# Linear-attention block on one core: out products of the full and the pooled half issued by turns, and the next-but-one strip's convolution moved between the kv products

## The chip, the core and the metric

One Trainium2 chip, one of its cores. The metric is the device time of one execution in microseconds (us). The kernel before takes 805.83 us, the median of three runs (805.62 to 808.54). All arithmetic is fp32.

## What is computed

The input x has shape (4, 128, 96, 96). It is normalised by group (32 groups of 4 channels) and then goes through a linear attention over 4x4 windows. Cut to what matters:

```python
qkv = einsum('nchw,oc->nohw', xw, qkv_w)            # xw: windows of 4x4 pixels of the normalised x
pooled = avg_pool5(qkv)                             # 5x5 mean inside the 4x4 window, zero padded
msq = concatenate([qkv, pooled], axis=1)            # a "full" half and a "pooled" half, 16 heads of 8 each
q, k, v = relu(msq[..., :8]), relu(msq[..., 8:16]), msq[..., 16:]    # v gets a ninth column of ones
kv  = einsum('ngld,nglm->ngdm', k, v)               # the kv products, 8 x 9 for each window and head
out = einsum('ngld,ngdm->nglm', q, kv)              # the out products
out = out[..., :-1] / (out[..., -1:] + 1e-15)
y = einsum('nchw,oc->nohw', out, proj_w)            # the projection of both halves
y = y * inv + shift                                 # batch norm
result = x + y
```

Pooling a 4x4 window by 5x5 leaves only 3x3 different values, so the kernel keeps 9 pixels of a window in the pooled half.

## The kernel before, in words

The image is cut into 96 strips of 4 rows (24 windows, 384 pixels, 216 pooled pixels). A strip s goes through these steps. Each bears the name of the helper in the code, and its engine:

- GpSimd (POOL), `normalise_and_pool(s)`: subtracts the mean (line 289), multiplies by 1/std (line 294, `xn_ready`) and adds up the 3x3 pooled sums (line 267, `xp_ready`). It waits for `q_p` of strip s-2, since `xn` and `xp` have two buffers each.
- TensorE (PE): `conv_kv(s)` (line 681) and `conv_kv_pooled(s)` (line 690) make k and v, `conv_q_full(s)` (line 706) and `conv_q_pooled(s)` (line 716) make q, all of them on the whole 128x128 array. `kv_products(s)` and `kv_products_pooled(s)` (both line 728) use tiles of 64x64 of the array. The out products (line 740) use tiles of 64 rows by 32 columns: 48 matmuls for each half, and the profile records every fp32 matmul as two MATMUL and two LDWEIGHTS. `project_full(s)` (line 797) and `project_pooled(s)` (line 805) are again on the whole array.
- ScalarE (ACT): `relu_q`, `relu_q_pooled` (line 384), `masked_v_full`, `masked_v_pooled` (line 365), `relu_k`, `relu_k_pooled` (lines 347 and 348) move the convolutions out of PSUM with relu and masks, `copy_y_pooled` (line 407) takes the pooled projection.
- VectorE (DVE): `own_heads` (line 565) masks the kv products into `kvc_full` and `kvc_pool`, `divide` (lines 594, 595, 598) divides the out products, `turn` (line 607) transposes them, `residual` (line 571) adds the full projection to x. On 72 of the strips it also takes the statistics of two strips of the next image (line 459).
- GpSimd again, `residual_pooled(s)` (line 267): adds the pooled projection; then the SyncE queue stores the strip.

PSUM has eight banks and is full: bank 6 holds the pooled k and v (`KV_P`), and later the full q (`Q_F`); bank 7 holds the pooled q and the pooled out products; the pooled kv products use banks 4 and 5, and bank 5 also holds the full out products. So `conv_kv_pooled` waits until ScalarE has read the full q of the strip before (`qm_f`), and `kv_products_pooled` waits until `divide` has read the full out products (`num_f`).

Every engine works through a fixed order, written by hand, one step per strip. On TensorE, step s of the kernel before is

```python
conv_kv(s + 1, p); conv_kv_pooled(s + 1, p); project(s - 1, out_next=True)
out_products(s); out_products_pooled(s)
kv_products(s + 1); kv_products_pooled(s + 1); conv_q(s + 1, p)
```

Strip 0 and the last one are written out, the others run in a hardware loop of two steps. On the other engines all 96 steps are written out. In a tile of the out products the rows come from the quad j of a half (64 partitions), the columns from the quad i of the output: i = 2g + j, so that the four matmuls of a window pair go to tiles (rows 0, columns 0), (rows 1, columns 1), (rows 0, columns 2), (rows 1, columns 3), in units of 64 rows and 32 columns.

Of the kernel before, what the change touches and what calls it, by code (L numbers as in the profile page):

```python
# [73 lines left out]
def build(nc, x, wq, wkv, proj, bn, consts, out):  # L74
# [24 lines left out]
    with ExitStack() as ctx:  # L99
        def sb(name, shape):  # L100
            return ctx.enter_context(nc.sbuf_tensor(name, [P, *shape], F32))
# [124 lines left out]
        def is_first(s):  # L226
            return isinstance(s, int) and s == 0
# [108 lines left out]
        def _(act):  # L336
# [18 lines left out]
            def relu_k_pooled(s):  # L355
                act.wait_ge(conv_p, s + 1)
                wait(act, kv_p, s)
                masked_k(k_pool, kv_tiles(KV_P, TP)[:, :, 0:P], C_KP).then_inc(km_p, 1)
# [9 lines left out]
            def masked_v_full(s, pairs=range(EF)):  # L368
                act.wait_ge(conv_f, s + 1)
                wait(act, kv_f, s)  # L370
                last = masked_v(vm_full, kv_tiles(KV_F, TF)[:, :, P:], pairs, C_VF)
                if EF - 1 in pairs:
                    last.then_inc(vm_f, 1)

            def masked_v_pooled(s):
                act.wait_ge(conv_p, s + 1)
                wait(act, kv_p, s)
                masked_v(vm_pool, kv_tiles(KV_P, TP)[:, :, P:], range(EP), C_VP).then_inc(vm_p, 1)
# [39 lines left out]
            def step(s, b, at, phase):  # L418
                if not is_first(s):
                    relu_q(s)  # L420
                    relu_q_pooled(s)
                if not is_first(s) and not is_last(s):
                    masked_v_full(s + 1)
                    relu_k(s + 1)
                if not is_last(s):
                    relu_k_pooled(s + 1)
                if not is_first(s):
                    copy_y_pooled(s - 1)
                if not is_last(s):
                    masked_v_pooled(s + 1)  # L430
                if phase == 3:
                    square_root(b + 1)

# [15 lines left out]
        def _(dve):  # L449
# [16 lines left out]
            def channel_stats(b):  # L466
                chained(dve.bn_aggr(mv[:, 0:2], stats[:].rearrange("p n c -> p (n c)")), b, 1)
# [88 lines left out]
            def own_heads(s, pooled):  # L556

                ready, free, done, bank, kvc = (
                    (kv_p, out_p, kvc_p, KVP, kvc_pool) if pooled else (kv_f, out_f, kvc_f, KVF, kvc_full))
                dve.wait_ge(ready, s + 1)  # L560
                wait(dve, free, s)
                shape = [P, 2, HALF, KC]
                own = col(C_OWN, KC).unsqueeze(1).unsqueeze(1).to_broadcast(shape)
                src = ps[:, bank:bank + 2, 0:HALF * KC].rearrange("p r (w c) -> p r w c", c=KC)
                dve.tensor_tensor(kvc[:], src, own, ALU.mult).then_inc(done, 1)  # L565

            def residual(s):
                dve.wait_ge(y_f, s + 1)
                xs = x_all[:, s * SP:(s + 1) * SP].rearrange("p (r w c) -> p r w c", r=WS, c=WS)
                ys = ps[:, Y_F, 0:SP].rearrange("p (w r c) -> p r w c", r=WS, c=WS)  # L570
                dve.tensor_tensor(xs, ys, xs, ALU.add).then_inc(added_f, 1)  # L571
# [29 lines left out]
            def turn(s, pooled):  # L601
                done, free, turned, o, o_t = (
                    (num_p, y_p, turned_p, o_pool, o_pool_t) if pooled else (num_f, y_f, turned_f, o_full, o_full_t))
                dve.wait_ge(done, s + 1)

                wait(dve, free, s)
                dve.transpose(o_t[:].rearrange("p n j -> p (n j)"),
                              o[:].rearrange("p n j -> p (n j)")).then_inc(turned, 1)

            def step(s, b, at, phase):  # L610
                own_heads(s, False)
                if phase == 0:
                    dve.wait_ge(gathered, b * FOURS + FOURS)
                own_heads(s, True)
                if is_first(s):
                    dve.wait_ge(proj_turned, 1)
                    dve.tensor_copy(projT[:], ps[:, PROJ_T, 0:2 * P]).then_inc(projT_ready, 1)
                if at is not None:
                    dve.wait_ge(loaded_later, 16 * (((b - 1) * SPB + at) // 2 + 1))
                    gather_strip(b, at)  # L620
                    last = gather_strip(b, at + 1)
                    if at % 4:
                        last.then_inc(gathered, 1)
                if phase == 0:
                    channel_stats(b)
                elif phase == 1:
                    group_average(b, 1)
                elif phase == 2:
                    group_mean(b)
                    group_average(b, 8)  # L630
                elif phase == 3:
                    group_var(b)
                elif phase == 4:
                    group_rstd(b, b + 2)
                if not is_first(s) and not is_last(s):
                    residual(s - 1)
                divide(s, False)
                if is_last(s):
                    turn(s, False)
                divide(s, True)  # L640
                if not is_last(s):
                    turn(s, False)
                turn(s, True)
                if is_last(s):
                    residual(s - 1)

            dve.wait_ge(loaded_w, 16 * 5)
            for e in range(EF):
# [13 lines left out]
            setup(dve.tensor_tensor(shift[:], bn_sb[:, 1:2], bn_off[:], ALU.subtract))  # L662
            dve.tensor_scalar(proj_sb[:], proj_sb[:], bn_inv[:], None, ALU.mult).then_inc(proj_scaled, 1)

            over_strips(step)
            residual(NS - 1)
            residual_pooled_last()

        @block.tensor
        def _(pe):  # L670
# [59 lines left out]
                                             start=True, stop=True)  # L730
                return last

            def out_products_of(q, kvc, bank, pairs):

                for n in range(HALF):
                    half, e = divmod(n, pairs)
                    for g in range(G):
                        for j in range(QG):
                            i, rows, z = g * QG + j, slice(H64 * j, H64 * (j + 1)), QS + n * QS + g * Q4
                            last = pe.matmul(ps[Q4 * i:Q4 * (i + 1), bank, n * KC:(n + 1) * KC], q[rows, z:z + Q4],  # L740
                                             kvc[rows, half % 2, (half // 2 * G + g) * pairs + e],
                                             start=True, stop=True)
                return last

            def kv_products(s):
# [29 lines left out]
                    pe.wait_ge(qm_p, s + 1)  # L775

            def out_products(s):
                if is_first(s) or is_last(s):
                    out_wait(s)
                    pe.nop(nofuse=True)  # L780
                out_products_of(q_full, kvc_full, OUTF_LAST if is_last(s) else OUTF, EF).then_inc(out_f, 1)

            def out_products_pooled(s):

                if is_last(s):
                    pe.wait_ge(kvc_p, s + 1)
                    pe.nop(nofuse=True)
                out_products_of(q_pool, kvc_pool, OUTP, EP).then_inc(out_p, 1)

            def project_full(s):  # L790
                pe.wait_ge(turned_f, s + 1)
# [20 lines left out]

            def step(s, p):

                if not is_first(s):
                    conv_kv(s + 1, p)
                    conv_kv_pooled(s + 1, p)
                    project(s - 1, out_next=True)
                out_products(s)
                out_products_pooled(s)  # L820
                if is_first(s):

                    pe.wait_ge(projT_ready, 1)
                kv_products(s + 1)
                kv_products_pooled(s + 1)
                conv_q(s + 1, p)

# [15 lines left out]
                last = pe.transpose(ps[:, PROJ_T, z * P:(z + 1) * P], proj_sb[:, z * P:(z + 1) * P], col(C_IDENT, P))  # L843
            last.then_inc(proj_turned, 1)


            step(0, 1)
            with pe.Fori(1, NS - 1, 2) as s:
                step(s, 0)
                step(s + 1, 1)  # L850
            out_products(NS - 1)
            project_full(NS - 2)
            out_products_pooled(NS - 1)
            project_pooled(NS - 2)
            project(NS - 1)


# [29 lines left out]
```

## Time and profile before

| | |
|---|---|
| median of three runs | 805.83 us |
| the profiled execution | 805.22 us |
| its span, first to last instruction | 803.4 us |
| TensorE clock granted, mean | 0.995 |
| busy: TensorE / VectorE / GpSimd / ScalarE | 766.7 / 622.8 / 591.6 / 567.4 us |
| one strip in the steady part | 7.91 us |

A group's time on TensorE is best read from the start of its first instruction to the start of the next group's first one, since matmuls overlap. "Idle before <-releaser" tells what an engine waited for; "issue" is a wait that the profile shows no cause for.

### The profile page before, as it was taken

Reading aid. Unit: us, or ns where it says so; the run is one execution under the profiler, and the core shown is the slowest. Engines: PE = TensorE matmul, PEld = TensorE weight load, DVE = VectorE, ACT = ScalarE, POOL = GpSimd, SP = SyncE. Lnnn points to the kernel's source line nnn. Section 1 sums busy time; section 2 is a strip of 40 time slices with the busy share of each in tenths; the row PEclk is TensorE's granted clock in tenths of the full one; section 3 lists DMA queues with packets and bytes.
Section 4 is the critical chain, followed back from the end, with each engine's and each line's share of the span. In section 5 each row is a group of like instructions: output and inputs, shape, how many; then the busy total and the mean of one; then the engine's idle time right before and its main releaser. Section 6 shows DMA issues by size and latency. Waiting matters only on the chain. (4 is left out here: it accounts for less than half of the span.)

```text
span 803.4 us, 62585 instructions
## 1 busy us (share of the span) xinstructions
PE 766.7 (95%) x28226; PEld 669.6 (83%) x28226; DVE 622.8 (78%) x1250; ACT 567.4 (71%) x1350; POOL 591.6 (74%) x1336
## 2 busy tenths in 40 slices
PE   0879999999999999999999999999999999999995
PEld 0668888888888888888888888888888888888884
DVE  7857888887768888888767888888777776767675
ACT  0557776768676777777676767677777767676773
POOL 0557877778787878787787878787877778787861
PEclk9999999999999999999999999999999999999998
DMA  7022131000012232000012222100000000000000
GB/s 298 3 63 59 59 89 40 30 29 21 29 59 82 66 89 59 30 20 30 23 47 70 77 75 74 49 20 29 20 30 20 30 26 24 30 20 30 20 30 31
DMA packets 20643, 38.74 MB, mean 48 GB/s; under 512 B 2416, under 2 KB 15216, under 8 KB 20592
## 3 DMA queue, kind: packets, MB, share of 16 engines
q1 hardware_dynamic: 20592, 38.25, 14.7%
q14 instruction: 42, 0.34, 0.1%
q8 instruction: 9, 0.15, 0.1%
HBM read 19.36 MB, written 18.87 MB: 48 GB/s over the span
## 5 line engine op out<-in xcount | busy, mean ns | idle before, releaser
L384 ACT ACTIVATE q_full<-ps,cst 128x384 f32<-128x384 f32 x192 | 103.7, 591 | 200.2 <-PE ps L706 200.2
L289 POOL TENSOR_TENSOR xd<-x_all,mean_t 128x384 f32<-128x384 f32 x95 | 78.8, 829 | 139.1 <-PE ps L716 119.3
L681 PE MATMUL ps<-wkv_sb,xn 128*128 128x256 f32 x576 | 142.9, 384 | 22.3 <-DVE xn L521 22.3
L267 POOL TENSOR_TENSOR x_all<-y_pool,x_all 128x96 f32<-128x96 f32 x380 | 148.2, 426 | 16.2 <-ACT y_pool L407 16.2
L681 PEld LDWEIGHTS ps<-wkv_sb,xn 128*128 128x128 f32 x576 | 102.9, 192 | 32.5 <-issue 22.3
L365 ACT ACTIVATE vm_pool<-ps,cst 128x256 f32<-128x256 f32 x288 | 119.5, 524 | 0.0
L571 DVE TENSOR_TENSOR x_all<-ps,x_all 128x384 f32<-128x384 f32 x96 | 53.5, 557 | 80.1 <-PE ps L797 80.0
L740 PEld LDWEIGHTS ps<-kvc_full,q_full 64*32 64x32 f32 x9216 | 88.1, 106 | 27.3 <-issue 27.3
L365 ACT ACTIVATE vm_full<-ps,cst 128x384 f32<-128x384 f32 x192 | 101.0, 579 | 4.6 <-PE ps L681 4.6
L740 PE MATMUL ps<-kvc_pool,q_pool 64*32 64x36 f32 x9216 | 100.3, 198 | 3.6 <-issue 3.6
L740 PE MATMUL ps<-kvc_full,q_full 64*32 64x36 f32 x9216 | 99.0, 198 | 1.5 <-ACT q_pool L384 1.5
L565 DVE TENSOR_TENSOR kvc_pool<-ps,cst 128x864 f32<-128x864 f32 x96 | 99.9, 1041 | 0.4 <-PE ps L728 0.4
L690 PE MATMUL ps<-wkv_sb,xp 128*128 128x256 f32 x384 | 99.0, 380 | 0.0
L565 DVE TENSOR_TENSOR kvc_full<-ps,cst 128x864 f32<-128x864 f32 x96 | 97.9, 1020 | 0.7 <-PE ps L728 0.7
L728 PE MATMUL ps<-vm_full,k_full 64*64 64x72 f32 x4608 | 95.2, 227 | 3.2 <-issue 3.2
L740 PEld LDWEIGHTS ps<-kvc_pool,q_pool 64*32 64x32 f32 x9216 | 90.8, 105 | 4.5 <-issue 4.4
L267 POOL TENSOR_TENSOR hs<-ht,xn 128x96 f32<-128x96 f32 x190 | 83.6, 440 | 14.9
L728 PE MATMUL ps<-vm_pool,k_pool 64*64 64x108 f32 x3072 | 89.3, 254 | 0.0
L706 PE MATMUL ps<-xn,wq_sb 128*128 128x192 f32 x384 | 89.3, 356 | 0.0
L728 PEld LDWEIGHTS ps<-vm_full,k_full 64*64 64x64 f32 x4608 | 80.5, 133 | 7.9 <-issue 3.5
L294 POOL TENSOR_TENSOR xn<-xd,rstd_t 128x384 f32<-128x384 f32 x95 | 78.5, 827 | 7.5
L690 PEld LDWEIGHTS ps<-wkv_sb,xp 128*128 128x128 f32 x384 | 73.0, 191 | 10.4 <-DVE xp L514 0.4
(72 smaller groups left out, 1414.6 us busy)
## 6 DMA issues: line engine op xcount, KB each, us to landing
out<-x_all SPq DMA_DIRECT2D x96, 192.0 KB, 1.9
x_all<-x SPq DMA_DIRECT2D x36, 384.0 KB, 3.3
x_all<-x SPq DMA_DIRECT2D x6, 768.0 KB, 8.2
wkv_sb<-wkv SPq DMA_DIRECT2D x1, 128.0 KB, 10.8
wq_sb<-wq SPq DMA_DIRECT2D x1, 128.0 KB, 10.6
proj_sb<-proj SPq DMA_DIRECT2D x1, 128.0 KB, 10.5
cst<-consts SPq DMA_DIRECT2D x1, 90.0 KB, 10.9
bn_sb<-bn SPq DMA_DIRECT2D x1, 2.0 KB, 10.3
```

What stands on the lines that cost most here:

```text
L267: return pool.tensor_tensor(o, a, b, ALU.add)
L289: link(pool.tensor_tensor(xd[:], x_all[:, s * SP:(s + 1) * SP], mean, ALU.subtract), 1)
L294: pool.tensor_tensor(xr, rows, rstd, ALU.mult).then_inc(xn_ready, 1)
L365: last = act.activation(heads[:, e, :, :, 0:D], src, ACT.Copy, scale=col(masks + e))
L384: return act.activation(to, src, ACT.Relu, scale=col(mask))
L565: dve.tensor_tensor(kvc[:], src, own, ALU.mult).then_inc(done, 1)
L571: dve.tensor_tensor(xs, ys, xs, ALU.add).then_inc(added_f, 1)
L681: last = pe.matmul(ps[:, bank, at:at + 2 * P], xn[:, p, t * P:(t + 1) * P], wkv_sb[:], start=True, stop=True)
L690: last = pe.matmul(ps[:, KV_P, t * 2 * P:(t + 1) * 2 * P], xp[:, p, t * P:(t + 1) * P], wkv_sb[:], start=True, stop=True)
L706: last = pe.matmul(ps[:, bank, PX + r * SP // PAIR:PX + (r + 1) * SP // PAIR], wq_sb[:, r], full[:, r], start=True, stop=True)
L728: last = pe.matmul(ps[H64 * j:H64 * (j + 1), bank + r, (t * G + g) * n:(t * G + g + 1) * n], k[rows, t, at:at + H64], vm[rows, :, t, i * K ...
L740: last = pe.matmul(ps[Q4 * i:Q4 * (i + 1), bank, n * KC:(n + 1) * KC], q[rows, z:z + Q4], kvc[rows, half % 2, (half // 2 * G + g) * pairs ...
```

## The change

1. The out products of both halves are issued by turns: the four matmuls of a window pair in the full half, then the four of the pooled half. The pooled ones have the two quads of a half swapped in their output place (i = 2g + 1 - j), so that they go to the four tiles that the full ones leave free; the columns of the projection weights are permuted to match, on the host. Both semaphores, `out_f` and `out_p`, are set at the end.
2. TensorE's step s is put in another order. `conv_kv` now runs for strip s+2 and stands between the full and the pooled kv products; `conv_kv_pooled(s + 2)` stands between the two projections of strip s.
3. ScalarE: `masked_v_full` runs for strip s+2, at the end of the step; `copy_y_pooled` comes ahead of `relu_k_pooled`.
4. VectorE: `divide` full, `divide` pooled, `own_heads(s+1)` full, `turn` full, `own_heads(s+1)` pooled, `turn` pooled, `residual(s)`; the statistics stand at the start of the step.
5. The hardware loop ends two strips earlier; the steps of strips 93 and 94 are written out.

```diff
-                    masked_v_full(s + 1)
                     relu_k(s + 1)
-                if not is_last(s):
-                    relu_k_pooled(s + 1)
                 if not is_first(s):
                     copy_y_pooled(s - 1)
                 if not is_last(s):
+                    relu_k_pooled(s + 1)
                     masked_v_pooled(s + 1)
+                if s < NS - 2:
+                    masked_v_full(s + 2)
...
+            def step(s, b, at, phase):
+                statistics(b, at, phase)
                 divide(s, False)
                 if is_last(s):
                     turn(s, False)
                 divide(s, True)
                 if not is_last(s):
+                    own_heads(s + 1, False)
                     turn(s, False)
+                    own_heads(s + 1, True)
                 turn(s, True)
-                if is_last(s):
-                    residual(s - 1)
+                residual(s)
...
+            def out_pair(q, kvc, bank, pairs, n, swap):
+                half, e = divmod(n, pairs)
+                for g in range(G):
+                    for j in range(QG):
+                        i, rows, z = g * QG + (1 - j if swap else j), slice(H64 * j, H64 * (j + 1)), QS + n * QS + g * Q4
...
             def out_products(s):
+                for n in range(HALF):
+                    full = out_pair(q_full, kvc_full, OUTF, EF, n, False)
+                    pooled = out_pair(q_pool, kvc_pool, OUTP, EP, n, True)
+                    if n == HALF - 1:
+                        full.then_inc(out_f, 1)
+                        pooled.then_inc(out_p, 1)
...
             def step(s, p):
-                if not is_first(s):
-                    conv_kv(s + 1, p)
-                    conv_kv_pooled(s + 1, p)
-                    project(s - 1, out_next=True)
+                convolved = not isinstance(s, int) or s < NS - 2
                 out_products(s)
-                out_products_pooled(s)
                 kv_products(s + 1)
+                if convolved:
+                    conv_kv(s + 2, p)
                 kv_products_pooled(s + 1)
-                conv_q(s + 1, p)
+                conv_q(s + 1, 1 - p)
+                project_full(s)
+                if convolved:
+                    conv_kv_pooled(s + 2, p)
+                project_pooled(s, out_next=True)
...
-            step(0, 1)
-            with pe.Fori(1, NS - 1, 2) as s:
-                step(s, 0)
-                step(s + 1, 1)
+            step(0, 0)
+            with pe.Fori(1, NS - 3, 2) as s:
+                step(s, 1)
+                step(s + 1, 0)
+            step(NS - 3, 1)
+            step(NS - 2, 0)
```

## Rows read from the trace of the kernel before

**Rows 1.** The page: busy time of each engine, its share of the span, instructions.
```profile
PE 766.7 (95%) x28226; PEld 669.6 (83%) x28226; DVE 622.8 (78%) x1250; ACT 567.4 (71%) x1350; POOL 591.6 (74%) x1336
```

**Rows 2.** Timeline, TensorE, one strip: start us, us, engine, line, operation, count.
```profile
400.44 0.92 PE L706 MATMUL ps<-xn,wq_sb 128*128 128x192 f32 x4
401.19 0.59 PE L716 MATMUL ps<-xp,wq_sb 128*128 128x108 f32 x4
401.62 1.47 PE L681 MATMUL ps<-wkv_sb,xn 128*128 128x256 f32 x6
402.93 1.03 PE L690 MATMUL ps<-wkv_sb,xp 128*128 128x256 f32 x4
403.80 0.81 PE L797 MATMUL ps<-o_full_t,projT 128*128 128x384 f32 x2
404.44 0.53 PE L805 MATMUL ps<-o_pool_t,projT 128*128 128x216 f32 x2
404.91 1.01 PE L740 MATMUL ps<-kvc_full,q_full 64*32 64x36 f32 x95
...
405.74 1.02 PE L740 MATMUL ps<-kvc_pool,q_pool 64*32 64x36 f32 x95
406.69 0.98 PE L728 MATMUL ps<-vm_full,k_full 64*64 64x72 f32 x48
407.50 0.92 PE L728 MATMUL ps<-vm_pool,k_pool 64*64 64x108 f32 x32
408.35 0.92 PE L706 MATMUL ps<-xn,wq_sb 128*128 128x192 f32 x4
```

**Rows 3.** Timeline cut at 404.96 (weight loads) and at 405.5 (matmuls).
```profile
404.90 0.15 PEld L740 LDWEIGHTS ps<-kvc_full,q_full 64*32 64x32 f32 x8 [0.27 <-issue]
404.91 0.78 PE L740 MATMUL ps<-kvc_full,q_full 64*32 64x36 f32 x68
```

**Rows 4.** Timeline, TensorE, before strip 0's out products.
```profile
28.17 0.98 PE L728 MATMUL ps<-vm_full,k_full 64*64 64x72 f32 x48
29.09 1.56 PE L681 MATMUL ps<-wkv_sb,xn 128*128 128x256 f32 x6
30.58 0.97 PE L728 MATMUL ps<-vm_pool,k_pool 64*64 64x108 f32 x32
31.48 1.13 PE L690 MATMUL ps<-wkv_sb,xp 128*128 128x256 f32 x4
32.45 0.38 PE L843 MATMUL ps<-cst,proj_sb 128*128 128x128 f32 x2
```

**Rows 5.** Timeline, ScalarE, the strip of rows 2.
```profile
401.39 1.08 ACT L384 ACTIVATE q_full<-ps,cst 128x384 f32<-128x384 f32 x2 [2.02 <-PE ps L706]
402.36 0.82 ACT L384 ACTIVATE q_pool<-ps,cst 128x216 f32<-128x216 f32 x2
```

**Rows 6.** Timeline, a TensorE instruction that waited for ScalarE, at the end.
```profile
797.37 0.44 ACT L407 ACTIVATE y_pool<-ps,shift 128x216 f32<-128x216 f32 x1 [6.77 <-issue]
...
797.96 1.21 PE L797 MATMUL ps<-o_full_t,projT 128*128 128x384 f32 x2 [2.48 <-ACT y_pool L407]
```

**Rows 7.** Timeline, VectorE, the strip of rows 2 and on.
```profile
405.98 0.21 DVE L594 TENSOR_SCALAR den_full<-ps 128x48 f32<-128x48 f32 x1 [0.78 <-PE ps L740]
...
407.18 0.20 DVE L594 TENSOR_SCALAR den_pool<-ps 128x48 f32<-128x48 f32 x1
...
408.38 0.57 DVE L607 STREAM_TRANSPOSE o_full_t<-o_full 128x384 f32<-128x384 f32 x1
...
409.33 1.02 DVE L565 TENSOR_TENSOR kvc_full<-ps,cst 128x864 f32<-128x864 f32 x1
...
410.27 1.04 DVE L565 TENSOR_TENSOR kvc_pool<-ps,cst 128x864 f32<-128x864 f32 x1
```

**Rows 8.** Timeline, TensorE, code of strip 0's step, then out products around the loop's end.
```profile
37.33 0.34 PE L728 MATMUL ps<-vm_full,k_full 64*64 64x72 f32 x4 [1.54 <-issue]
...
784.43 1.01 PE L740 MATMUL ps<-kvc_full,q_full 64*32 64x36 f32 x95
...
798.96 0.93 PE L805 MATMUL ps<-o_pool_t,projT 128*128 128x216 f32 x2
```

More of the change, by code:

```diff
@@ L608, in turn, with statistics @@
                               o[:].rearrange("p n j -> p (n j)")).then_inc(turned, 1)
[L610 to L617, printed above, removed]
+            def statistics(b, at, phase):
                 if at is not None:
@@ L624, in step @@
                 if phase == 0:
+                    dve.wait_ge(gathered, b * FOURS + FOURS)
                     channel_stats(b)
@@ L634, in step @@
                     group_rstd(b, b + 2)
-                if not is_first(s) and not is_last(s):
-                    residual(s - 1)
+            def step(s, b, at, phase):
+                statistics(b, at, phase)
                 divide(s, False)
@@ L641, in step @@
                 if not is_last(s):
+                    own_heads(s + 1, False)
                     turn(s, False)
+                    own_heads(s + 1, True)
                 turn(s, True)
-                if is_last(s):
-                    residual(s - 1)
+                residual(s)
             dve.wait_ge(loaded_w, 16 * 5)
@@ L663, in _ @@
             dve.tensor_scalar(proj_sb[:], proj_sb[:], bn_inv[:], None, ALU.mult).then_inc(proj_scaled, 1)
+            own_heads(0, False)
+            own_heads(0, True)
+            dve.wait_ge(proj_turned, 1)
+            dve.tensor_copy(projT[:], ps[:, PROJ_T, 0:2 * P]).then_inc(projT_ready, 1)
             over_strips(step)
-            residual(NS - 1)
             residual_pooled_last()
@@ L731, in kv_tile @@
                 return last
[L733 to L742, printed above, removed]
+            def out_pair(q, kvc, bank, pairs, n, swap):
[3 more added lines that the diff above has]
+                        i, rows, z = g * QG + (1 - j if swap else j), slice(H64 * j, H64 * (j + 1)), QS + n * QS + g * Q4
+                        last = pe.matmul(ps[Q4 * i:Q4 * (i + 1), bank, n * KC:(n + 1) * KC], q[rows, z:z + Q4],
+                                         kvc[rows, half % 2, (half // 2 * G + g) * pairs + e],
+                                         start=True, stop=True)
                 return last
@@ L777, in out_products, with out_products_last @@
             def out_products(s):
-                if is_first(s) or is_last(s):
+                if is_first(s):
                     out_wait(s)
                     pe.nop(nofuse=True)
-                out_products_of(q_full, kvc_full, OUTF_LAST if is_last(s) else OUTF, EF).then_inc(out_f, 1)
-            def out_products_pooled(s):
-                if is_last(s):
-                    pe.wait_ge(kvc_p, s + 1)
-                    pe.nop(nofuse=True)
-                out_products_of(q_pool, kvc_pool, OUTP, EP).then_inc(out_p, 1)
+                for n in range(HALF):
[4 more added lines that the diff above has]
+                        pooled.then_inc(out_p, 1)
+            def out_products_last(s, pooled):
+                if pooled:
+                    pe.wait_ge(kvc_p, s + 1)
+                else:
+                    out_wait(s)
+                pe.nop(nofuse=True)
+                for n in range(HALF):
+                    last = (out_pair(q_pool, kvc_pool, OUTP, EP, n, True) if pooled else
+                            out_pair(q_full, kvc_full, OUTF_LAST, EF, n, False))
+                last.then_inc(out_p if pooled else out_f, 1)
             def project_full(s):
@@ L844, in _ @@
             last.then_inc(proj_turned, 1)
-            step(0, 1)
-            with pe.Fori(1, NS - 1, 2) as s:
-                step(s, 0)
-                step(s + 1, 1)
[L851 to L854, printed above, removed]
+            step(0, 0)
[4 more added lines that the diff above has]
+            step(NS - 2, 0)
+            out_products_last(NS - 1, False)
+            out_products_last(NS - 1, True)
             project(NS - 1)
@@ L869 @@
     wq = np.stack([quads, quads[:, ::-1]], axis=1).transpose(0, 1, 3, 2, 4).reshape(P, PAIR, P)
-    proj = np.asarray(L0_conv_proj_w).reshape(P, 2 * P)
+    proj = np.asarray(L0_conv_proj_w).reshape(P, 2, G, QG, Q4).copy()
+    proj[:, 1] = proj[:, 1, :, ::-1]
+    proj = np.ascontiguousarray(proj.reshape(P, 2 * P))
     arrays = {
```

## The prediction

> **What bounds the kernel now.** I read the page's busy shares first, then one strip of the timeline engine by engine, then the first strips. TensorE is busy for 95% of the span and no other engine for more than 78% [rows 1]. In a strip of 7.91 us (from one conv_q at 400.44 to the next at 408.35) its groups follow each other without a hole [rows 2]: conv_q 0.75 and 0.43, conv_kv 1.31, its pooled half 0.87, the projections 0.64 and 0.47, the out products 0.83 and 0.95, the kv products 0.81 and 0.85. ScalarE waits 2.02 us in the same strip for TensorE, and VectorE at least 0.78 [rows 5, 7]. So a strip costs what TensorE's own chain costs, and the change pays if that chain gets shorter. It must not put a wait into it.
>
> **The out products by turns.** From the first record to the last they take 1.66 us for 192 matmul records (404.91 to 406.57; the last start is the kv products' start at 406.69 less a hand-over of 0.13) [rows 2]. That is 8.6 ns a record, while only four of the eight 64x32 tiles work. With all eight in turn a record no longer waits for its own tile, and what is left is how fast records come. Two rows bound that. At the start of the group eight weight loads go out in 0.055 us, with four matmuls among them: about 6.7 ns for a load and its matmul [rows 3]. That burst is the fastest in the trace; at its pace 192 records take 1.30 us with the start-up. The other bound is today's 1.66. After the burst the first 68 records have gone by 405.5, 8.7 ns each, and the other 124 take the remaining 1.07 us, 8.6 ns each [rows 2, 3]: it never again comes near 6.7. The loads, far ahead of the matmuls in the first slice (eight loads to five matmuls), have no lead worth the name later. An engine that waits for a tile would have its loads done ahead; one that waits for instructions would look like this. So I take the supply of instructions as the limit of the long part, and from the extra tiles only the gain in the first part: 1.60 us, a gain of 0.06 us a strip. That nothing is gained is the upper bound (1.66), 1.30 the lower one of this reading.
>
> The Trainium skill speaks for more. Its page "TensorE: Matmul & The Clock Gate", Part 3, has matmuls on different tiles start about 4 ns apart, by which 192 records would take 0.77 us. No stretch of this trace goes at that pace, and the fastest one has 6.7 ns; it is one of the rivals below.
>
> **The new place of conv_kv.** Between the two kv products the array changes from 64x64 tiles to the whole array and back, which the kernel before does not do in the steady part. But it does so once, ahead of strip 0 [rows 4]: full kv 28.17, conv_kv 29.09, pooled kv 30.58, next group 31.48. There the full kv products cost 0.91 where a steady strip has 0.81, conv_kv 1.49 against 1.31, the pooled kv products 0.90 against 0.85 [rows 2, 4]. The sum is 0.34 us a strip more. None of it hides, since TensorE is the chain. It could be less if some of those 0.18 us in conv_kv were a wait for VectorE's or ScalarE's first-strip work; I put its lower bound at 0.2.
>
> **The new place of conv_kv_pooled.** It still waits for `qm_f`, both parts of relu_q, because it writes bank 6. Today conv_q pooled (0.43) and conv_kv (1.31) stand between conv_q_full and it; afterwards conv_q pooled and project_full (0.64). TensorE gets to it 0.75 + 0.43 + 0.64 = 1.82 us after conv_q_full starts. relu_q starts 0.95 us after conv_q_full starts (400.44 to 401.39) and takes 1.08 [rows 2, 5]: 2.03 us. The hand-over from ScalarE to TensorE took 0.15 us where TensorE waited for it (797.81 to 797.96) [rows 6]. So conv_kv_pooled starts at 2.18 instead of 1.82: a new wait of 0.36 us in every strip. Behind an empty array the group also takes longer: conv_kv_pooled took 0.97 (31.48 to 32.45) after a change of tiles against 0.87 [rows 2, 4], 0.10 more. Together 0.45 us. Queued behind it are the pooled projection and the next out products; relu_q_pooled, which the pooled projection waits for, ends at 402.36 + 0.82 = 403.18, 2.74 us after conv_q_full, and conv_kv_pooled (0.87 after 2.18, so 3.05 and more) covers it [rows 5].
>
> **What doesn't bind.** VectorE now has divide full, divide pooled and one own_heads ahead of the full turn. A divide takes 1.20 us from start to start (405.98, 407.18, 408.38), the two turns 0.95, an own_heads 0.94 [rows 7]. After the last out record: 0.24 + 1.20 + 1.20 + 0.94 + 0.57 + 0.1, that is 4.25 us to project_full. TensorE gets there after 0.13 + 0.91 + 1.49 + 0.90 + 0.75 + 0.43 = 4.61. To the pooled projection VectorE needs 0.24 + 2.40 + 1.88 + 0.95 + 0.1 = 5.6, TensorE 4.61 + 0.64 + 0.36 + 0.97 = 6.6. The full divide (1.5 us to its end, to be done before the pooled kv products) is covered by full kv and conv_kv, 2.5 us. ScalarE works 5.9 us in a strip, moves masked_v_full into its idle time ahead of relu_q and is free there; GpSimd's strip is unchanged and starts from `q_p` as before, with xn ready 1.8 us later and needed after about 5. Were one of these covers gone, its cost would be the difference of the two numbers named. These edits I cost at nothing.
>
> **Edges.** Strips 93 and 94 are now straight code. Strip 0's step, also straight code, lost 1.54 us in the middle of its kv products to nothing the profile names but issue [rows 8]; for two such steps I add 3.2 us (bounds 0 and 8). In the tail of the kernel before, the last pooled projection starts 14.5 us after strip 94's out products (784.43 to 798.96) [rows 8]. In the new order VectorE's chain sets it, about 7.7 us to the last out products and 5 behind them: 1.5 us less.
>
> **The sum.** Per strip +0.34 + 0.45 - 0.06 = +0.73 us, so 8.64 us a strip. It applies to some 92 strips (1 to 93, less one for the first pass through the loop's code, where other waits cover it): +67.4. With the edges (+3.2 - 1.5) it is +69.1. The profiled execution of before takes 805.2 us, 0.6 below the median, so it gives 874.3 as a profiled execution and **875** as a median.
>
> **The rivals.**
> - Records come at the burst's pace all through (6.7 ns). For it: the burst exists and eight tiles free the array. Against: 8.6 ns later without the loads' lead. Out products 1.30: +0.43 x 92 + 1.7 = +41, **847**.
> - The new wait does not appear, because relu_q starts earlier or bank 6 is free sooner than I read. For it: only that its size, 0.45, is a difference of longer terms. +0.28 x 92 + 1.7 = +27, **833**.
> - The turns do nothing at all: two tiles in the same rows or the same columns don't stream together. In today's out products a group of 64 rows feeds two column tiles at once, and afterwards it would have to feed four, which no row shows. +0.79 x 92 + 1.7 = +74, **880**.
> - Faster: all eight tiles stream together, and eight records take what four take now. Then the out products take half of 1.66, 0.83. The change breaks even at 1.66 - 0.79 = 0.87 us, 4.5 ns a record; below that it gains. At 0.83 it gives -4 + 2, that is 804; at 0.78 and without the restart of 0.10, -0.19 x 92 + 1.7 = -16, 790. I take **796**. Against it is that even the burst, with nothing in its way, took 6.7 ns. By the skill's 4 ns (0.77 us, as above) it would be an estimated 800.
>
> **How the numbers follow.** Forecast 0.48, burst's pace 0.20, no wait 0.09, turns without effect 0.10, eight tiles together 0.13. The predicted time is the forecast's. The range goes from 832 to 886: it takes in the first four cases, with the bounds of the edges. A change of 0.5%, 4 us, is about what a measurement can tell from none. Faster by more: 0.10, out of the last rival; within 0.5%: 0.04, the rest of it and the low ends of the others; slower: 0.86.
>
> **What would show it.** In the profile of the changed kernel a strip should take 8.6 us; the waits should show conv_kv_pooled (line 690 of before) waiting for ScalarE's q_full, some 90 times 0.4 to 0.5 us; the out products should take 1.6 us from first to last; conv_kv should take 1.49 from its start to the pooled kv products. Out products well under 1.3 us would prove my reading of the instruction supply wrong, and under 0.87 the sign with it. A wait of TensorE for VectorE ahead of a projection would show a chain that I counted as covered.

## The result

The changed kernel takes 878.3 us, the median of four runs (877.03 to 879.85), against 805.7 for the kernel before on the same chip: slower by a factor of 1.090 (95% interval 1.0879 to 1.0921). Forecast were 875, and 832 to 886. The profiled execution spans 874.5 us from its first to its last instruction, where the kernel before has 803.4; the mean granted clock is 0.995 in both.

The profile's timeline of one steady strip of the changed kernel on TensorE (start us, us, engine, line, operation, count; most rows of the out products, from 402.22 up to 403.98, are left out where the "..." stands):

```profile
399.83 0.82 PE L808 MATMUL ps<-o_full_t,projT 128*128 128x384 f32 x2
400.82 1.10 PE L690 MATMUL ps<-wkv_sb,xp 128*128 128x256 f32 x4 [0.17 <-ACT q_full L385]
401.75 0.54 PE L816 MATMUL ps<-o_pool_t,projT 128*128 128x216 f32 x2
402.22 0.24 PE L740 MATMUL ps<-kvc_full,q_full 64*32 64x36 f32 x4
...
403.98 0.98 PE L728 MATMUL ps<-vm_full,k_full 64*64 64x72 f32 x48
404.89 1.56 PE L681 MATMUL ps<-wkv_sb,xn 128*128 128x256 f32 x6
406.38 0.97 PE L728 MATMUL ps<-vm_pool,k_pool 64*64 64x108 f32 x32
407.29 0.92 PE L706 MATMUL ps<-xn,wq_sb 128*128 128x192 f32 x4
408.04 0.59 PE L716 MATMUL ps<-xp,wq_sb 128*128 128x108 f32 x4
408.47 0.82 PE L808 MATMUL ps<-o_full_t,projT 128*128 128x384 f32 x2
409.46 1.10 PE L690 MATMUL ps<-wkv_sb,xp 128*128 128x256 f32 x4 [0.17 <-ACT q_full L385]
```

Read it from start to start and against [rows 2]. From one project_full to the next it is 8.64 us, where a strip took 7.91. (Read finer, the out products of 90 successive strips start 8.647 us apart, those of the kernel before 7.907.) The whole difference stands in five places: full kv products 0.91 (0.81 before), conv_kv 1.49 (1.31), pooled kv products 0.91 (0.85), project_full to conv_kv_pooled 0.99 (0.64 for the same projection), conv_kv_pooled 0.94 (0.87). The out products gave back 0.02 to 0.03: 1.76 to the first kv product, against 1.78.

Who waited for whom, in the changed kernel (engine, line, releaser: us in total, times, longest):

```profile
DVE den_full L595 <- PE ps L740: 220.3, 96, 4.8
ACT vm_full L366 <- PE ps L681: 192.0, 95, 5.0
POOL xd L290 <- PE ps L716: 188.6, 94, 8.5
PEld ps L690 <- issue: 70.9, 94, 0.8
...
PE ps L690 <- ACT q_full L385: 15.9, 94, 0.2
```

Every other engine waits longer for TensorE than before: VectorE 220 us against 152, GpSimd 189 against 119, ScalarE 263 against 200. The one new wait of TensorE's in the loop is 94 times line 690, the pooled convolution, for ScalarE's relu_q. The 0.17 us of the matmul's row is only what was left after the matmul before it had drained; the weight loads' row, 70.9 us over 94, 0.75 each, shows how long the loads had stood. The real price is the difference in start times, 0.35 us a strip.

Around the loop's end, the changed kernel's timeline on TensorE (the first row is of strip 93's step and the next two of strip 94's, both now straight code; the last two are of the last strip):

```profile
847.54 0.27 PE L728 MATMUL ps<-vm_full,k_full 64*64 64x72 f32 x1 [1.60 <-issue]
...
855.48 0.35 PE L728 MATMUL ps<-vm_full,k_full 64*64 64x72 f32 x6
857.78 0.86 PE L728 MATMUL ps<-vm_full,k_full 64*64 64x72 f32 x41 [1.95 <-issue]
...
867.72 0.91 PE L808 MATMUL ps<-o_full_t,projT 128*128 128x384 f32 x2
869.82 1.09 PE L816 MATMUL ps<-o_pool_t,projT 128*128 128x216 f32 x2 [1.18 <-DVE o_pool_t L608]
```

### The profile page after: what moved, and what is told of

It reads as the page before. It is cut to its first block, busy times and chain, and to the rows that moved or that the text cites. A ratio compares the mean times of both kernels' runs of the same rounds, so it can differ in the third digit from the quotient of the medians.

```text
span 874.5 us, 62720 instructions
## 1 busy us (share of the span) xinstructions
PE 820.5 (94%) x28226; PEld 659.1 (75%) x28226; DVE 621.5 (71%) x1250; ACT 580.0 (66%) x1350; POOL 590.3 (68%) x1336
## 4 chain that ended last, share of the span: by engine, by line
PE 82%; issue 8%; ACT 7%; DVE 2%; DMA 0%; ACTq 0%; DVEq 0%
PE ps L728 20%; PE ps L740 19%; PE ps L681 17%; PE ps L690 12%; PE ps L706 10%; ACT q_full L385 7%; PE ps L816 4%; DVE stats L460 1%; DMA x_all<-x 0%; ACTq L213 0%; PE ps L716 0%; DVE mv L468 0%; PE ps L808 0%; DVE x_all L585 0%; DVE o_pool_t L608 0%
## 5 line engine op out<-in xcount | busy, mean ns | idle before, releaser
L740 PE MATMUL ps<-kvc_pool,q_pool 64*32 64x36 f32 x9216 | 173.1, 205 | 4.2 <-issue 4.2
L595 DVE TENSOR_SCALAR den_full<-ps 128x48 f32<-128x48 f32 x96 | 19.9, 207 | 220.3 <-PE ps L740 220.3
L740 PEld LDWEIGHTS ps<-kvc_full,q_full 64*32 64x32 f32 x9216 | 156.2, 105 | 26.2 <-issue 25.9
L681 PE MATMUL ps<-wkv_sb,xn 128*128 128x256 f32 x576 | 151.4, 399 | 22.0 <-DVE xn L522 22.0
L740 PE MATMUL ps<-kvc_full,q_full 64*32 64x36 f32 x9216 | 169.0, 205 | 0.0
L740 PEld LDWEIGHTS ps<-kvc_pool,q_pool 64*32 64x32 f32 x9216 | 153.5, 105 | 4.5 <-issue 4.5
L690 PEld LDWEIGHTS ps<-wkv_sb,xp 128*128 128x128 f32 x384 | 65.1, 189 | 76.4 <-issue 70.9
L690 PE MATMUL ps<-wkv_sb,xp 128*128 128x256 f32 x384 | 105.9, 398 | 15.9 <-ACT q_full L385 15.9
L728 PEld LDWEIGHTS ps<-vm_pool,k_pool 64*64 64x64 f32 x3072 | 73.6, 133 | 31.5 <-issue 31.5
L728 PE MATMUL ps<-vm_pool,k_pool 64*64 64x108 f32 x3072 | 93.7, 260 | 0.0
```

Of the source, the lines that this page charges most:

```text
L595: link(dve.tensor_scalar(den[:], src[:, :, D], DEN_EPS, None, ALU.add), s, step + 1)
L681: last = pe.matmul(ps[:, bank, at:at + 2 * P], xn[:, p, t * P:(t + 1) * P], wkv_sb[:], start=True, stop=True)
L690: last = pe.matmul(ps[:, KV_P, t * 2 * P:(t + 1) * 2 * P], xp[:, p, t * P:(t + 1) * P], wkv_sb[:], start=True, stop=True)
L728: last = pe.matmul(ps[H64 * j:H64 * (j + 1), bank + r, (t * G + g) * n:(t * G + g + 1) * n], k[rows, t, at:at + H64], vm[rows, :, t, i * K ...
```

## The experiments

All times stand beside runs of the kernel before on the same chip, 805.4 to 806.1 us. "A strip" is the median distance from one strip's first out product to the next one's.

**Which part costs what: the order alone.** The changed kernel, with its out products as before (one half after the other, on four tiles, with the projection weights not permuted; "..." marks lines left out of a diff).

```diff
                 for n in range(HALF):
                     full = out_pair(q_full, kvc_full, OUTF, EF, n, False)
-                    pooled = out_pair(q_pool, kvc_pool, OUTP, EP, n, True)
-                    if n == HALF - 1:
-                        full.then_inc(out_f, 1)
-                        pooled.then_inc(out_p, 1)
+                full.then_inc(out_f, 1)
+                for n in range(HALF):
+                    pooled = out_pair(q_pool, kvc_pool, OUTP, EP, n, False)
+                pooled.then_inc(out_p, 1)
...
```

> The changed kernel with its new order, but with the out products one half after the other and on the tiles of the kernel before. Theory (long out-product streams are paced by the supply of instructions, not by tiles): the out products go from 1.64 to 1.66 us a strip, the whole from 878.3 to 880 us (878 to 882). Rival (eight tiles at work are what keeps the new order from being worse): the out products lose 0.3 us or more, 905 us or more.

Measured: 880.3 us, 1.092 (1.089 to 1.094) of before, 8.673 us a strip. The turns are worth 0.026 us a strip of the changed kernel, some 2 us in all, which is inside the spread of the runs but plain in the strip. The order makes the whole loss: with it alone a strip takes 0.766 us more than before.

**The turns alone.** The kernel before in its own order, with the turns, the swap and the permuted weights.

```diff
-                out_products_of(q_full, kvc_full, OUTF_LAST if is_last(s) else OUTF, EF).then_inc(out_f, 1)
...
+                for n in range(HALF):
+                    full = out_pair(q_full, kvc_full, OUTF, EF, n, False)
+                    pooled = out_pair(q_pool, kvc_pool, OUTP, EP, n, True)
+                full.then_inc(out_f, 1)
+                pooled.then_inc(out_p, 1)
...
```

> The kernel before with the turns alone (swapped quads, permuted projection weights), its order untouched. Theory: the out products gain 0.02 us a strip, but the full ones are now done 0.8 us later, and the pooled kv products wait for divide full: last out record + 0.24 + 1.28 + 0.15, that is 3.30 us after the first out record where they started after 2.59; with a restart of 0.07 it is +0.78 x 94 = 73, 879 us (872 to 886). Rival (VectorE is early enough, the turns cost nothing): 804 us.

Measured: 866.2 us, 1.074 (1.072 to 1.077), 8.560 a strip. The wait is there, in every strip. Timeline of this kernel, first VectorE, then TensorE:

```profile
607.15 0.21 DVE L594 TENSOR_SCALAR den_full<-ps 128x48 f32<-128x48 f32 x1 [1.51 <-PE ps L738]
...
607.88 0.56 DVE L598 TENSOR_TENSOR o_full<-ps,den_full 128x384 f32<-128x384 f32 x1
```

```profile
607.11 0.98 PE L728 MATMUL ps<-vm_full,k_full 64*64 64x72 f32 x48
608.54 0.97 PE L728 MATMUL ps<-vm_pool,k_pool 64*64 64x108 f32 x32 [0.45 <-issue]
```

The pooled kv products start 1.43 us after the full ones, not 0.80, just when divide full ends (607.88 + 0.56 = 608.44, and 0.10 of hand-over). The profile puts this wait down to "issue"; that it is for divide full is read from these times, and the 0.10 from the divide's end to the pooled kv products is the same in every steady strip. I had put the pooled kv products 0.11 later; so the loss is 60 us and not 73. The mechanism held, the sum was too large. The run also shows what the new place of conv_kv is good for: it fills this very hole, 0.65 us a strip. But it costs 0.34 a strip, and with the 0.42 that the new place of conv_kv_pooled costs, no less than the hole.

**The wait for relu_q.** The changed kernel with conv_q_full moved ahead of the pooled kv products.

```diff
                 if convolved:
                     conv_kv(s + 2, p)
+                pe.wait_ge(vm_p, s + 2)
+                conv_q_full(s + 1, 1 - p)
                 kv_products_pooled(s + 1)
-                conv_q(s + 1, 1 - p)
+                conv_q_pooled(s + 1, 1 - p)
```

> The changed kernel with conv_q_full moved ahead of the pooled kv products (it waits for vm_p there), so that ScalarE's relu_q starts some 0.9 us earlier and is done when the pooled convolution comes. Theory: the wait of 0.35 us and the restart of 0.07 a strip vanish: 8.23 us a strip, 878 - 0.42 x 92 = 839 us (834 to 846). Rival (the wait only moves, to VectorE's turn or to ScalarE's masked_v_full, which now stands ahead of relu_q): 860 us or more.

Measured: 841.4 us, 1.044 (1.042 to 1.047), 8.238 a strip. Its timeline on TensorE shows no wait ahead of line 690, and conv_kv_pooled takes 0.87 again (from start to start):

```profile
607.65 0.82 PE L808 MATMUL ps<-o_full_t,projT 128*128 128x384 f32 x2
608.31 1.03 PE L690 MATMUL ps<-wkv_sb,xp 128*128 128x256 f32 x4
609.18 0.53 PE L816 MATMUL ps<-o_pool_t,projT 128*128 128x216 f32 x2
```

So the wait and the restart behind it were 0.41 of the 0.74 us a strip, and 37 of the 73 us.

**The change of tiles.** The changed kernel with conv_kv ahead of both kv products: the array changes its tiles once less in a strip, and every group and nearly every wait stays.

```diff
+                if convolved:
...
+                        pe.wait_ge(y_copied, s)
+                    conv_kv(s + 2, p)
                 kv_products(s + 1)
-                if convolved:
-                    conv_kv(s + 2, p)
                 kv_products_pooled(s + 1)
```

> The changed kernel with conv_kv ahead of the full kv products instead of between the two, so that the array changes its tiles four times a strip and not five; the wait for relu_q stays. Theory (a change of tiles costs by itself): one change less, 0.11 (exit of the full kv) + 0.06 (restart of the pooled kv) = 0.17 x 92 = 16 us less, 862 us (858 to 868). Rival (the 0.34 us are the semaphore waits and the queueing of these groups, which are all still there): 876 us or more.

Measured: 863.5 us, 1.071 (1.068 to 1.074). The strips alternate, 8.485 and 8.549 us (a few 8.58): the loop's body holds two strips, and it is always the same one of the two that is longer. Timeline on TensorE, one strip of each kind:

```profile
603.49 1.56 PE L681 MATMUL ps<-wkv_sb,xn 128*128 128x256 f32 x6
604.98 0.98 PE L728 MATMUL ps<-vm_full,k_full 64*64 64x72 f32 x48
605.78 0.92 PE L728 MATMUL ps<-vm_pool,k_pool 64*64 64x108 f32 x32
606.63 0.92 PE L706 MATMUL ps<-xn,wq_sb 128*128 128x192 f32 x4
...
611.97 1.56 PE L681 MATMUL ps<-wkv_sb,xn 128*128 128x256 f32 x6
613.47 0.98 PE L728 MATMUL ps<-vm_full,k_full 64*64 64x72 f32 x48
614.28 0.97 PE L728 MATMUL ps<-vm_pool,k_pool 64*64 64x108 f32 x32
615.18 0.92 PE L706 MATMUL ps<-xn,wq_sb 128*128 128x192 f32 x4
```

In the shorter strips the full kv products are back at 0.80 and the pooled ones at 0.85, 0.16 less than in the changed kernel. In the others the full ones take 0.81, but the pooled ones still 0.90, and the gain is 0.10; so a change of tiles is not the only thing that costs a group its restart, and what it is there the rows don't tell. conv_kv takes 1.49 in its new place too, behind the out products' tiles. So one change of tiles less gave 0.16 us in one strip of two and 0.10 in the other, 0.13 on average and not the 0.17 of the theory. That the total came so near to the expected 862 is in part luck: from strip 93's out products on the run takes 28.7 us, where the changed kernel takes 31.3. The rival, waits and queueing alone (876 or more), is out; what is changed besides the tiles is only which group stands behind which.

**Both.** conv_kv and conv_q_full ahead of both kv products.

```diff
+                if convolved:
...
+                    conv_kv(s + 2, p)
+                pe.wait_ge(vm_p, s + 2)
+                conv_q_full(s + 1, 1 - p)
                 kv_products(s + 1)
-                if convolved:
-                    conv_kv(s + 2, p)
                 kv_products_pooled(s + 1)
-                conv_q(s + 1, 1 - p)
+                conv_q_pooled(s + 1, 1 - p)
```

> Both at once: conv_kv and then conv_q_full ahead of both kv products. Theory: the two costs add up, 878 - 39 - 16 = 823 us (818 to 830); what is left over the kernel before is one change of tiles a strip more. Rival (with conv_q_full so early another chain ends last, VectorE's turns ahead of the projections or ScalarE's masked_v_full ahead of relu_q): 835 us or more.

Measured: 870.7 us, 1.080 (1.077 to 1.083), 8.625 a strip: the rival was right. Its timeline, VectorE first, then TensorE:

```profile
611.95 1.06 DVE L566 TENSOR_TENSOR kvc_full<-ps,cst 128x864 f32<-128x864 f32 x1 [0.67 <-PE ps L728]
612.92 0.57 DVE L608 STREAM_TRANSPOSE o_full_t<-o_full 128x384 f32<-128x384 f32 x1
```

```profile
610.90 0.98 PE L728 MATMUL ps<-vm_full,k_full 64*64 64x72 f32 x48
...
613.54 0.91 PE L808 MATMUL ps<-o_full_t,projT 128*128 128x384 f32 x2 [0.30 <-DVE o_full_t L608]
```

The two convolutions ahead of the kv products take 2.1 us (608.75 to 610.90 by their starts), so the full ones end later; own_heads full stands ahead of the turn on VectorE and waits for them (0.67), and project_full waits for the turn. By their starts project_full comes 1.00 us after conv_q pooled, where it came 0.43 after it: the two gains are given back by this one wait. In the changed kernel project_full had 0.4 us in hand there, by the working of the prediction and by its own rows; I had not asked what a later kv product does to it.

**What paces the out products.** Four kernels. First, the changed kernel without the swap (and without the permuted weights), so that both halves by turns use the same four tiles:

```diff
-                    pooled = out_pair(q_pool, kvc_pool, OUTP, EP, n, True)
+                    pooled = out_pair(q_pool, kvc_pool, OUTP, EP, n, False)
```

> The changed kernel, full and pooled still by turns, but the quads not swapped, so that both halves use the same four tiles. Theory: tiles matter only in the first burst; the burst is as in the kernel before (about 8.1 ns a record for some 36 records), the rest at 8.3 ns; 880 us. Rival (the swap is what the turns need): the stream is slower than 1.66 us a strip, 885 us or more.

Measured: 880.5 us, 1.094 (1.090 to 1.097), a strip of 8.647, that of the changed kernel. The time is as expected, the strip is not: 880 us stood for out products of 1.66, and they take 1.635 from first to last record, as in the changed kernel (1.661 before and with the order alone). The time was hit by chance: in the profiled executions the first three strips take 36.1 us here and 32.8 in the changed kernel. By the records' starts the two kernels with turns lack a pause of 0.026 us that the others have at about record 130. The eight tiles put the changed kernel 0.017 us ahead by record 64 (0.551 against 0.568), and it loses that again in the last eight records. What little the turns gain is therefore not the tiles' doing.

Second, half the moving columns, then half the stationary ones, with as many instructions (each leaves out a part of the out products):

```diff
-                        last = pe.matmul(ps[Q4 * i:Q4 * (i + 1), bank, n * KC:(n + 1) * KC], q[rows, z:z + Q4],
-                                         kvc[rows, half % 2, (half // 2 * G + g) * pairs + e],
+                        last = pe.matmul(ps[Q4 * i:Q4 * (i + 1), bank, n * KC:n * KC + KC // 2], q[rows, z:z + Q4],
+                                         kvc[rows, half % 2, (half // 2 * G + g) * pairs + e, 0:KC // 2],
```

> The changed kernel with out matmuls of 18 instead of 36 columns (heads 3 and 4 of each quad of the out products are left out). Theory (supply of instructions): as many instructions, so the long stretch stays at 8.3 ns a record and the out products at 1.63 us; 878 us. Rival (the array or its moving operand sets the pace): the stream gets faster, towards 1.30 us or less; 847 us or less.

```diff
-                        last = pe.matmul(ps[Q4 * i:Q4 * (i + 1), bank, n * KC:(n + 1) * KC], q[rows, z:z + Q4],
+                        last = pe.matmul(ps[Q4 * i:Q4 * i + Q4 // 2, bank, n * KC:(n + 1) * KC], q[rows, z:z + Q4 // 2],
```

> The changed kernel with out matmuls of 16 instead of 32 stationary columns (one window of each pair is left out of the out products), moving columns as before. Theory (supply of instructions): as many instructions, out products still 1.63 us a strip, 878 us. Rival (the weight loads set the 8.3 ns a record, 64 rows by 32 columns each): the long stretch gets up to twice as fast, 840 us or less.

Measured: 877.6 and 877.6 us, strips of 8.613 and 8.618. Half the columns or half the weights change the out products by 0.03 us in 1.76, to the first kv product. From the pooled projection to the first kv product, by their starts, it is 2.19 us in both, against 2.23 in the changed kernel (401.75 to 403.98):

```profile
603.46 0.53 PE L816 MATMUL ps<-o_pool_t,projT 128*128 128x216 f32 x2
605.65 0.98 PE L728 MATMUL ps<-vm_full,k_full 64*64 64x72 f32 x48
```

```profile
600.86 0.53 PE L816 MATMUL ps<-o_pool_t,projT 128*128 128x216 f32 x2
603.05 0.98 PE L728 MATMUL ps<-vm_full,k_full 64*64 64x72 f32 x48
```

(The first fence is the kernel with half the columns, the second the one with half the weights.) Last, half the instructions over as many columns (every second window pair gets the query of the one before it):

```diff
-                for n in range(HALF):
+                for n in range(0, HALF, 2):
...
-                        last = pe.matmul(ps[Q4 * i:Q4 * (i + 1), bank, n * KC:(n + 1) * KC], q[rows, z:z + Q4],
-                                         kvc[rows, half % 2, (half // 2 * G + g) * pairs + e],
+                        last = pe.matmul(ps[Q4 * i:Q4 * (i + 1), bank, n * KC:(n + 2) * KC], q[rows, z:z + Q4],
+                                         kvc[rows, half % 2, at:at + 2].rearrange("p w c -> p (w c)"),
```

> The changed kernel with half as many out matmuls, each over 72 instead of 36 moving columns: as many columns through the tiles, half the instructions (the second window pair of each two gets the query of the first, so those outputs are left out). Theory (supply of instructions): the 96 records end where record 96 of the changed kernel stands, 0.82 us after the first, instead of 1.63: 0.8 us a strip less, 7.85 us, some 805 us. Rival (columns set the pace after all): 1.5 us or more, 870 us.

Measured: 807.0 us, 1.002 (1.001 to 1.004), 8.027 a strip. The out products take 1.14 us to the first kv product instead of 1.76 (604.57 + 0.46 to 606.17):

```profile
604.57 0.54 PE L817 MATMUL ps<-o_pool_t,projT 128*128 128x216 f32 x2
606.17 0.98 PE L728 MATMUL ps<-vm_full,k_full 64*64 64x72 f32 x48
```

From the first to the last record they take 0.99, not the 0.82 of the theory and far from the 1.5 of the rival. The difference is in the burst: with 72 columns eight records take 62 ns, with 36 columns the changed kernel has 24 out in 127 ns; and the stream has a second gap of about 0.05 us. Between the gaps the records come at 8.4 to 8.6 ns, nearly the pace of before.

The strip is 0.12 us longer than that of the kernel before, 11 us over the 90 strips in the middle, and not 0.06 shorter, as the expectation had it. The total came within 2 us of the kernel before, and of the expectation, because the first three strips take 26.3 us here and 32.1 there: with fewer instructions TensorE stalled there once, for 1.70 us, and not three times. So the out products confirm the theory, and the total is a hit by luck.

## Why the prediction came out

**The out products.** The step that the sign hung on was that the long part of the stream is paced by the supply of instructions. The four runs bear it out: neither half the columns nor half the weights nor the choice of tiles moves it by more than 0.03 us, half the instructions do.

The sign that I had read it from does not bear it out, though. I had compared the loads' lead over the matmuls, eight to five in the first slice [rows 3], and called it gone later. The timeline of the kernel before cut at 405.5 has this row beside the 68 matmuls of [rows 3]:

```profile
404.90 0.70 PEld L740 LDWEIGHTS ps<-kvc_full,q_full 64*32 64x32 f32 x71 [0.27 <-issue]
```

71 to 68 is a lead of three, as in the first slice. So in the kernel before the lead tells nothing of what changes between the burst and the stream; the conclusion was right, and this ground for it was not. In the changed kernel the lead does fall, from seven loads in the burst to 1.5 on average from record 40 on.

How it looks in the changed kernel, in counts of line 740's matmuls up to 402.35, 402.46 and 402.9 (operation, count, durations in ns, first and last start; the group starts at 402.22):

```profile
L740 PE MATMUL ps<-kvc_full,q_full x14: 195/197/218, 402.2 to 402.3; 64*32 64x36 f32 x14
...
L740 PE MATMUL ps<-kvc_pool,q_pool x11: 194/198/218, 402.2 to 402.3; 64*32 64x36 f32 x11
...
L740 PE MATMUL ps<-kvc_full,q_full x16: 195/196/218, 402.2 to 402.4; 64*32 64x36 f32 x16
...
L740 PE MATMUL ps<-kvc_pool,q_pool x16: 194/196/218, 402.2 to 402.4; 64*32 64x36 f32 x16
...
L740 PE MATMUL ps<-kvc_full,q_full x41: 189/198/218, 402.2 to 402.9; 64*32 64x36 f32 x41
...
L740 PE MATMUL ps<-kvc_pool,q_pool x38: 194/198/218, 402.2 to 402.9; 64*32 64x36 f32 x38
```

By 402.35, 0.13 us in, 25 records are out. By 402.46 there are 32, and not one came after 402.39: the burst is over and the gap has begun. By 402.9 there are 79, that is 47 in 0.44 us, 9.4 ns each with the rest of the gap, and the other 113 take 0.95 us, 8.5 each, 8.3 but for the end. This is the 0.06 of the sum, which measured 0.026. I had let the burst's gain stand, and the gap behind it takes nearly all of it back: at record 31 the changed kernel is 0.10 us ahead of the kernel before, at record 64 0.02. That instructions are what runs out, and not some other thing that goes with their number, such as a fixed cost of each load with its matmul, stays an inference: no run shows the queue.

One step here was wrong, though it didn't show in the time. I took the burst of [rows 3], 6.7 ns a record, for the pace at which records can come at best. In the changed kernel 24 records start in 0.127 us, 5.3 ns each: the first 14 at 6.7 ns, the next ten within 0.04. In the kernel before, the fifth record comes 33 ns after the fourth, and from there on four tiles give 8.1 ns, so its trace could not show the faster pace. So 1.30 us was no lower bound: had the supply held at 5.3 ns, the out products would have come to 1.02, not far from break-even (0.87). The Trainium skill's page "TensorE: Matmul & The Clock Gate", Part 3, has about 4 ns from tile to tile. This trace agrees with that for the last eight of those 24 records (4.3 ns each), and for no long stretch: for the whole stream, at 1.635 us, the 0.77 of that reckoning is farther off than my 1.30.

**conv_kv between the kv products.** +0.34 was forecast from strip 0's rows [rows 4] and +0.34 measured, group by group (0.911, 1.492, 0.901). A row of the same order in a corner of the old trace was worth more than any reckoning. Of this, 0.16 in one strip of two and 0.10 in the other went away with one change of tiles less, in the run with conv_kv first. conv_kv's own 0.18 stayed in that run. With conv_q_full behind it conv_kv takes 1.40, but conv_q pooled then takes 0.54 instead of 0.43, so that nothing of it came back there either.

**conv_kv_pooled's wait.** Forecast 0.36 and 0.10 of restart; measured 0.35 (0.991 against 0.645) and 0.07 (0.938 against 0.864). In the run with conv_q_full early both are gone (0.660 and 0.863), and the other groups together take the same within 0.01. The second rival, that the wait is not there, falls.

**The covers**, the waits that I had counted as hidden behind TensorE's own work, held in the changed kernel: apart from the start, where it waits 22.0 us for the first normalised input, TensorE waits for VectorE only once, at the end (the last row of the fence on the loop's end). The turn that project_full needs ends at 407.96, and project_full starts at 408.47, so 0.4 us are left with a hand-over of 0.1:

```profile
407.39 0.57 DVE L608 STREAM_TRANSPOSE o_full_t<-o_full 128x384 f32<-128x384 f32 x1
```

That is closer than "costs nothing" says, as the run with both moves shows.

**The edges.** Strips 93 and 94, in straight code, took 20.7 us from the first one's out products to the last strip's, where they took 14.2: +6.5. From there to the end it is 2.1 less. Forecast were +3.2 and -1.5, together off by 2.7. Strip 93 lost 1.9 us, 1.60 of them in one stall; strip 94 stalled for 1.95 (the rows on the loop's end), and behind the stall the granted clock was lower, which I had not priced. The windows view (length, busy and count of TensorE, its loads, VectorE, ScalarE, GpSimd, then the granted clock, the DMA share and GB/s) before and after the end of that stall:

```profile
853.70:857.80 4.10, 2.15 (x203) 1.94 (x203) 2.14 (x6) 2.36 (x7) 1.56 (x4) 1.00 0.15 52
857.80:862.00 4.20, 4.20 (x82) 3.94 (x82) 3.17 (x5) 0.53 (x2) 0.00 (x0) 0.62 0.01 4
```

A mean of 0.62 is mostly 1.2 GHz and partly 2.4; conv_q takes 1.44 us there instead of 0.75. TensorE had stood still for 1.95 us before.

**The sum** in the profiled executions: 90 x 0.74 = 66.6, +6.5 - 2.1, and 0.1 at the start, 71.1 us; forecast 69.1. The rivals by the burst's pace (847), by no wait (833) and by eight tiles streaming (796) are out; "the turns do nothing" (880) differs from what happened only by 0.026 us a strip. Its reason was wrong, though: in the last experiment a tile gets its next 72 columns every 62 ns as long as the burst lasts, with eight tiles in turn, where with four tiles it gets 36 in 32.5 ns. So all eight tiles do stream together. After the burst they had nothing to stream.

The waits and groups came out one by one, but that the sum is so near is in part luck. A strip's 0.74 against 0.73 hides a gain from the turns put 0.03 too high against a wait and a restart put 0.03 too high together; and the edges' 2.7 us too little stand against two strips too many, 1.5 us. In the recorded working 0.36 and 0.10 make 0.46, not 0.45, and 92 times 0.73 is 67.2, not 67.4; both slips are rounding and change nothing.

## What to carry to other kernels

A stream of small tiled matmuls can be limited by how fast its instructions come; then more tiles at work change next to nothing (0.03 us of 1.66 here, and none of it the tiles' doing). The test that told it was to halve the columns, the weights and the instructions one at a time; the loads' lead over the matmuls did not tell it in the kernel before. Before a step is moved on a full engine, price two things from rows: what the array loses at each new change of tiles, and whose result the step will reach earlier than today. An order that fills one hole is only worth it if it costs less than the hole, and here filling 0.65 us cost 0.76.

## What the runs showed of the hardware

- Matmul records of 64x32 tiles in fp32, each with its weight load, start 5.3 ns apart in a burst of 32 when eight tiles take part (8.1 with four, 7.8 with eight and 72 columns). With eight tiles a gap of 0.08 us follows (0.06 with 72 columns), with four none. Behind it come 8.3 ns a record, with 18 or 36 moving columns, 16 or 32 stationary ones, four tiles or eight.
- Two changes more between tiles of 64x64 and the whole array cost 0.34 us a strip on a chain that is full; one less gave back 0.16 us in one strip of two and 0.10 in the other.
- TensorE stalled for "issue" by 1.5 to 2 us in code that it ran for the first time: in the changed kernel once in each of strips 0 (1.54), 1 (1.76), 2 (1.79), 93 (1.60), 94 (1.95) and 95 (1.80), and never from the loop's second pass to its end. Behind the stall of 1.95 us the granted clock fell to a mean of 0.62 over 4.2 us. Why it stalls no run shows.
